# Attention's residual added by VectorE, the turned input copied in halves, and the first source ids loaded ahead of three rows

## The reference

```python
# layer 0: attention over the graph, then a feed-forward part
q, k, v = x @ Wq + bq, x @ Wk + bk, x @ Wv + bv        # 8 heads of 64
attn = softmax(where(adj == 0, -1e9, q k^T / 8))       # over the axis of heads
h1 = layer_norm(x + (attn v) @ Wo + bo, g1, be1)
ff = relu(h1 @ W1 + b1) @ W2 + b2
x1 = layernorm(x + layer_norm(h1 + ff, g2, be2))
# layer 1: messages along the edges
h = mish(concat(x1[src], x1[dst], edge_attr) @ W1 + b1)
messages = mish(h @ W2 + b2)
agg = segment_sum(messages, dst)                       # and so on
```

## Time and profile before

| | |
|---|---|
| median of 3 runs | 235.0 us (234.98 to 235.89) |
| the profiled execution's own time | 235.0 us |
| its span, first to last instruction | 233.2 us |
| outside the span | 1.8 us |
| PE busy | 223.6 us, 96% of the span |
| DVE busy | 174.2 us, 75% |
| ACT busy | 125.6 us, 54% |
| granted TensorE clock, mean | 0.992 |

### The profile page before, as it was taken

The page is one execution under the profiler, slowest core; times in us unless marked ns, Lnnn a source line. Parts: engine busy times, 40 slices in busy tenths (PEclk is TensorE's granted clock), DMA queues, the critical chain, the costliest instruction groups (busy, mean ns, idle before and its releaser), DMA issues.

```text
span 233.2 us, 3303 instructions
## 1 busy us (share of the span) xinstructions
PE 223.6 (96%) x1217; PEld 181.1 (78%) x1217; DVE 174.2 (75%) x313; ACT 125.6 (54%) x232; POOL 5.5 (2%) x17
## 2 busy tenths in 40 slices
PE   8999999999999999999999999999999999999970
PEld 4985789766766887888888888888888888997770
DVE  3979776497797688876967868877778767868634
ACT  0645589449679537635646537457475535722300
POOL 1000010000000000000000000000000000001001
PEclk9999999999999999999999999999999999999996
DMA  6999999994004827136100000069830000000001
GB/s 219 292 397 387 397 389 394 404 371 199 1 0 174 364 43 118 23 56 107 19 1 3 0 0 1 0 224 310 292 121 0 0 3 1 0 3 0 0 3 45
DMA packets 28615, 31.26 MB, mean 134 GB/s; under 512 B 17948, under 2 KB 18868, under 8 KB 27576
## 3 DMA queue, kind: packets, MB, share of 16 engines
q1 hardware_dynamic: 27808, 30.54, 38.8%
q10 hardware_dynamic: 792, 0.51, 0.9%
HBM read 30.79 MB, written 0.26 MB: 133 GB/s over the span
## 4 chain that ended last, share of the span: by engine, by line
PE 74%; DMA 9%; SPq 6%; DVE 5%; issue 2%; ACTq 2%; POOL 1%; ACT 1%; POOLq 0%; DVEq 0%
PE bank L735 37%; PE bank L718 13%; DMA ids<-in_src 5%; SPq L240 5%; PE bank L525 4%; DMA Wc<-in_L_gnn_W 3%; PE bank L745 3%; PE bank L534 3%; PE bank L746 3%; PE bank L566 2%; SPq L257 2%; PE bank L694 1%; PE bank L595 1%; PE bank L695 1%; PE bank L699 1%
## 5 line engine op out<-in xcount | busy, mean ns | idle before, releaser
L735 PE MATMUL bank<-W2hi,Hhi 128*128 128x512 f32 x128 | 49.8, 389 | 0.0
L735 PE MATMUL bank<-W2hi,Clo 128*128 128x512 f32 x128 | 49.8, 389 | 0.0
L735 PE MATMUL bank<-W2lo,Hhi 128*128 128x512 f32 x128 | 49.8, 389 | 0.0
L433 ACT ACTIVATE Mhi<-M 128x512 fp32r<-128x512 f32 x32 | 20.3, 634 | 44.2 <-DVE M L1128 44.2
L1133 DVE TENSOR_TENSOR Mlo<-M,Mhi 128x512 fp32r<-128x512 f32 x32 | 22.1, 690 | 11.8 <-ACT M L434 11.8
L1128 DVE TENSOR_TENSOR M<-bank,b2r 128x512 f32<-128x512 f32 x32 | 22.0, 687 | 10.3 <-PE bank L746 5.5
L735 PEld LDWEIGHTS bank<-W2hi,Hhi 128*128 128x128 f32 x128 | 24.0, 188 | 5.0
L735 PEld LDWEIGHTS bank<-W2lo,Hhi 128*128 128x128 f32 x128 | 24.0, 188 | 5.0
L735 PEld LDWEIGHTS bank<-W2hi,Clo 128*128 128x128 f32 x128 | 24.0, 188 | 5.0
L426 ACT ACTIVATE Hhi<-C 128x512 fp32r<-128x512 f32 x32 | 20.0, 624 | 11.3 <-DVE C L1114 11.1
L340 ACT ACTIVATE C<-bank,cols 128x512 f32<-128x512 f32 x32 | 19.5, 704 | 10.5 <-PE bank L566 10.5
(11 more groups left out here) (246 smaller groups left out, 333.5 us busy)
## 6 DMA issues: line engine op xcount, KB each, us to landing
F<-in_L_gnn_W SPq DMA_DIRECT2D x2, 2048.0 KB, 20.7
W<-in_L_gnn_W SPq DMA_DIRECT2D x3, 1024.0 KB, 5.4
W1raw<-in_L_gnn_W SPq DMA_DIRECT2D x1, 2048.0 KB, 23.2
ids<-in_src SPq DMA_DIRECT2D x2, 1024.0 KB, 13.5
ids<-in_dst SPq DMA_DIRECT2D x2, 1024.0 KB, 6.6
dst_ids<-in_dst SPq DMA_DIRECT2D x2, 1024.0 KB, 7.5
src_ids<-in_src SPq DMA_DIRECT2D x1, 2048.0 KB, 8.0
Wq<-in_L_gnn_Wq SPq DMA_DIRECT2D x4, 256.0 KB, 3.9
```

Source lines behind the costliest of these rows:

```text
L433: act.activation(Mhi[:, t, :], M[:, t, :], ACT.Mish)
L735: done = mm(ST2[t][:, :], x[:, c, e], w[:, c, :], start=c == 0 and i == 0, stop=c == KC - 1 and i == 2)
```

## The change

Three parts. `start_with` and its two products are gone; the bias product at L627 now opens the two output banks (`start=True`), and the statistics of the banks are replaced by the helper `residual` with `xs` as the tile to add. The four transposes of the input go in pairs into `bank[1]` and `bank[3]`, each pair with its own signal and its own copy by VectorE, and the product with `Wq` waits for the second half only at its third piece. On SyncE's queue the first half of the source ids stands ahead of the three rows, behind the wait for `wo_done`.

```diff
             sp.dma_start(F2, w_view(a["L0_gnn_W2"])).then_inc(S["f2_in"], 16)
-            for name in EARLY_ROWS[2:]:
-                load_row(name)
             sp.wait_ge(S["wo_done"], 2)
             for h in range(2):
                 sp.dma_start(other[f"ids{h}"], by_partition(...)).then_inc(S[f"row_ids_in{h}"], 16)
+                if h == 0:
+                    for name in EARLY_ROWS[2:]:
+                        load_row(name)
...
-            transpose4(bank[1], xs, S["x_transposed"])
-            start_with(O_BANKS, xs)
+            for h in range(2):
+                for c in range(2):
+                    done = nc.tensor.transpose(quarter((bank[1], bank[3])[h], c), xs[:, P * (2 * h + c):P * (2 * h + c + 1)], ident[:, :])
+                done.then_inc(S["x_transposed"], 1)
             pe.wait_ge(S["xT_ready"], 1)
...
                 for c in range(KC):
+                    if c == 2:
+                        pe.wait_ge(S["xT_ready"], 2)
...
-                mm(O_BANKS[b][:, 0:D // 2], ones2[:, :], bvo_parts[...], start=False, stop=False)
+                mm(O_BANKS[b][:, 0:D // 2], ones2[:, :], bvo_parts[...], start=True, stop=False)
...
-            dve.wait_ge(S["x_transposed"], 1)
-            v.tensor_copy(xT_flat, bank[1][:, :]).then_inc(S["xT_ready"], 1)
+            for h in range(2):
+                dve.wait_ge(S["x_transposed"], h + 1)
+                v.tensor_copy(half(xT_flat, h), (bank[1], bank[3])[h][:, 0:D // 2]).then_inc(S["xT_ready"], 1)
...
-            st = bank_statistics(O_BANKS, S["wo_done"])
-            norm_gain(O_BANKS, y[:, :], r("L0_gnn_g1"), r("L0_gnn_be1"), S["nx_ready"], st)
+            st = residual(O_BANKS, xs, S["wo_done"])
+            norm_gain(y[:, :], y[:, :], r("L0_gnn_g1"), r("L0_gnn_be1"), S["nx_ready"], st)
```

More of the change, by code:

```diff
@@ L501, in _ @@
             mm = nc.tensor.matmul
[L503 to L507, removed]
             def transpose_halves(banks, src, ready, before, signal):
@@ L515, in transpose_halves @@
                     done.then_inc(signal, 1)
-            def start_with(banks, x):
-                for h in range(2):
-                    mm(banks[h][:, 0:D // 2], ident[:, :], half(x, h), start=True, stop=False)
             def columns_by(banks, lhs, rhs, h, cs, start, stop):
@@ L626, in _ @@
             for b in range(2):
-                mm(O_BANKS[b][:, 0:D // 2], ones2[:, :], bvo_parts[:, D + D // 2 * b:D + D // 2 * (b + 1)], start=False, stop=False)
+                mm(O_BANKS[b][:, 0:D // 2], ones2[:, :], bvo_parts[:, D + D // 2 * b:D + D // 2 * (b + 1)], start=True, stop=False)
             for h in range(2):
```

## The result

The changed kernel takes 235.95 us (median of 20 executions, 235.24 to 236.31), the kernel before in the same sessions 235.24 us (20 executions, 234.88 to 235.97). The ratio (of means) is 1.002, with a 95% interval of 1.001 to 1.0029: 0.2 to 0.7 us slower, about half a microsecond in the middle. The profiled execution has a span of 233.9 us against 233.2.

A forecast was written before the change was run, and what follows sets the result against it. VectorE's path and ScalarE's evictions, ending within 0.1 us of each other, bound layer 1's first weight load, with TensorE gapless behind. Start 0, eviction path +0.47: 235.0 + 0.47 = 235.5 us, range 234.6 to 236.2.

The forecast's parts named there:

- The time: Whole kernel: 235.5 us, 0.2% more than before, below the 0.5% a measurement can tell from no change.
- The ids are worth nothing at the end: At layer 1's first products: earlier ids alone save 0.30 us on VectorE's path, nothing on the eviction path.
- The predicted wait of about 1 us for the second half: Behind the first one-hot matrix: VectorE, through at 45.2 us, waits for the second half of the ids until 46.25.
- The eviction path sets the weight load: At layer 1's start: ScalarE's bank evictions behind F2 release the first weight load at 56.00 us, 0.47 later.
- The tie with VectorE's path: At layer 1's first products: VectorE's path and ScalarE's evictions end within 0.1 us of each other.
- The first norm costs 0.47 us: At the first norm: VectorE's steps end 0.72 us later, slack hides part, the first feed-forward product starts 0.47 later.
- my upper bound of 0.72: At the first norm: the cost in us if nothing of VectorE's delay is hidden.
- The start is worth 0: At the start: product with Wq begins 0.3 to 0.6 us earlier, but the scores stay at 13.3 us.
- the cover: Ahead of the scores: Wchi's 1.54 us wait for its transfer hides the start's gain of up to 0.6 us.
- The clock as a rival: At the start: TensorE idles, its clock falls to 1.2 GHz for the product with Wq, 238.8 us; chance 0.05.
- this sign: In the first 15 us: a granted clock below 1.00 would show the forecast wrong.

The follow-up runs named there:

- p_ids: Kernel before with only SyncE's queue changed, the first half of the source ids ahead of the three rows; ratio 1.0005.
- e_fill: Kernel before without the two identity products, with two warming products behind the transposes, ahead of the product with Wq; ratio 0.9988.
- e_poollate: Kernel before with a small GpSimd memset ahead of the root of the second norm; 235.45 us in one execution.
- d_before: Kernel before with an extra 512-column VectorE addition ahead of the second residual; 23.60 us from first feed-forward product to layer 1's first weight load, one execution.
- e_poolwarm: Changed kernel with one small GpSimd multiplication at about 23.5 us, ahead of the roots; 235.42 us in one execution.
- e_wide: Kernel before without the two identity products, with one more wait ahead of the product with Wq; ratio 1.005.
- p_halves: Kernel before with only the turned input copied in halves, the identity products kept behind the transposes; ratio 0.9988, median 234.99 us.
- v_both: Kernel before with the input in halves and the ids moved, without the residual on VectorE; ratio 0.9991, median 235.15 us.
- e_nostart: Kernel before without the two identity products, attention's residual left out of the sum; ratio 1.0015, median 235.14 us.
- e_gap: Changed kernel with a one-column VectorE memset between the aggregation and the gain of the first norm; ratio 1.0002 to the kernel before.
- v_split: Kernel before with halves and moved ids, residual kept on TensorE, its identity products moved to waits for ScalarE; ratio 0.9991, median 235.18 us.
- p_resid: Kernel before with only attention's residual moved to VectorE; ratio 1.004, median 236.02 us.

## Why the prediction was right, by its steps

- **The time.** Predicted 235.5 us and 0.2% more; measured a ratio of 1.002. The direction, the size and the side of the 0.5% are right. The size is so in part by luck: two terms of the sum were off by 0.44 and 0.25 us, in opposite directions.
- **The ids are worth nothing at the end**: right within 0.1% or so, and shown by p_ids (1.0005, B unchanged), with the reservation of e_fill, where the late ids cost 0.2 us. The landings came at 27.48 + 13.3 = 40.8 and 31.43 + 13.8 = 45.2 us, 1.1 us ahead of the predicted ones, because the queue as a whole was ahead in this execution; the lead of one half over the other, 4.4 us, is the predicted 4.3. The predicted wait of about 1 us for the second half did not come: VectorE lost 1.00 us earlier, waiting for ScalarE's rounded part of `W1`, which I had not counted, and the second half was there (45.2) when VectorE was ready for it (45.39). VectorE's wait for F2 is 2.11 us and not 0.9, because its second addition was ready about 1 us sooner than predicted, and F2 came 0.25 us later.
- **The eviction path sets the weight load**: right. It was released by ScalarE in the profile after, at 56.18 against a predicted 56.00. The tie with VectorE's path is shown by e_poollate for an execution with late ids, and d_before showed that it is no property of every execution; in e_fill VectorE's path even ends last by 0.2 us.
- **The first norm costs 0.47 us**: the mechanism was right and its own size too: with a root of 0.55 us A is 5.13 in e_poolwarm, 0.46 more than before, and the root-and-shift step there begins 2.92 us behind the norm's start, as I had added it up. What was missing is the root. I took "from there to the gain 0.27, from the gain to the next step 0.81" from the second norm, where GpSimd starts 0.05 us behind the gain, and did not ask whether it would at the first, where it starts 0.12 us behind. That is 5.58 - 5.13 = 0.45 us more, and the term is 0.91 us, beyond my upper bound of 0.72.
- **The start is worth 0**: mis-sized. Wc's transfer, which I named as the cover, let ScalarE begin Wchi at 12.38 in the one profile before, but at 11.20 in the profile after and between 10.92 and 12.17 in all other profiles except e_wide's. So the cover is thin; the profile after has 0.25 us of gain. It made up for half of the unseen cost of the root. No experiment with twelve executions tells this gain from nothing: p_halves and v_both have 0.9988 and 0.9991, with intervals that reach 1. Two errors of opposite sign met in a sum that was nearly right.
- **The clock as a rival**, at 0.05: the long form did not happen in 20 executions of the changed kernel, but its profile shows a short one: the first few products with Wq at half pace, 0.39 us, in the one place that I had named. Without the identity products and without the halves, 5 of 12 executions were 1.8 us longer, and the profile of e_wide shows the half pace in a long execution, 1.87 us lost in the product with Wq. I argued against it from the tail, where a gap keeps the clock; that says little about a clock that has only just risen or has yet to. I also looked for it in the granted clock, which reads 1.00 in the first 15 us of every profile here, slow products or not, so that this sign could not have shown it. In the changed kernel the weight loads pause for 0.49 us ahead of the product with Wq, against 1.02 in e_nostart, and the products for 0.08 against 0.78. That the halves protect it by this fits 0 long executions of 20 in the change and 0 of 12 in e_gap, but v_split, whose start is the same, has 1 of 12, and p_resid without the halves only 2 of 12. It was not tried by itself.

## What to carry to other kernels

A chain of waits that runs through a transfer prices that transfer only until the next arrival: look up who else is waiting at the place where the chain meets the bounding engine, before crediting the wait. When an operand moves from PSUM to SBUF, count the SBUF inputs of the VectorE instruction and look for GpSimd instructions that start beside it; 0.1 us of order there cost 0.45 us, as much as the two additions that the change was about. And do not take one profile's slack for cover: the landing of the transfer that was to hide the start moved by more than a microsecond from execution to execution.

## What the runs showed of the hardware

- GpSimd's root of 128 numbers, eight of them in each of the 14 profiles, took 0.55 or 0.56 us in all but three cases (1.04, 1.04, 1.08), each with a VectorE instruction of two SBUF inputs started 0.08 to 0.12 us before it. The slow ones ended about 0.4 us behind that instruction (29.88 to 30.29).
- The work between the warming products and the first real ones changes the spread of times. The same two identity products took 1.03 us in the profile before, 1.65 in d_before and 1.91 us in p_ids:

```profile
4.45 1.91 PE L521 MATMUL bank<-xs,ident 128*128 128x256 f32 x4
```

  and the kernel before itself has executions near 235.0 and near 235.7 us, a difference of similar size. That the start makes these two groups fits the profiles but was not shown.
- The first issue behind the load of F2 took 9.63 us when it stood there at 20.3 us, and 1.96 us when it was held back to 27.5 us; what stood behind it was issued at nearly the same time either way (31.84 and 31.43 us for the second half of the ids).
